# A third context load behind two gathers, and its transposes behind two products

## The chip, the cores and the metric

The kernel runs on one core of a Trainium2 chip. The metric is the device time of one execution in microseconds; shown is the median of three. A profiled execution gives the trace that is read below. PE is TensorE, PEld its weight loads, DVE VectorE, ACT ScalarE, POOL GpSimd, SP SyncE.

## What is computed

A gated block of two parts, each with a layer norm ahead and a residual behind. First each of 2048 tokens goes through one of four experts, chosen by its token id. All three weight matrices of an expert are the same 512 x 512 context block:

```python
def _L0_xattn_ref(hidden_states, token_ids, Wg, Wu, Wd):      # Wg = Wu = Wd = ctx_2048
    expert_ids = jnp.minimum(tid // tokens_per_expert, E - 1)
    for e in range(E):
        g = jax.nn.silu(jnp.einsum('bsd,fd->bsf', hidden_states, Wg[e]))
        u = jnp.einsum('bsd,fd->bsf', hidden_states, Wu[e])
        y = jnp.einsum('bsf,df->bsd', g * u, Wd[e])
        out = jnp.where((expert_ids == e)[..., None], y, out)

x = x + jnp.tanh(g_xattn[0]) * _L0_xattn_ref(_layernorm(x), itok, ctx_2048, ctx_2048, ctx_2048)
x = x + jnp.tanh(g_ffn[0]) * _L0_ffn_ref(_layernorm(x), gate_W, W1, b1, W2, b2)
```

The second part picks two of six experts for each of the four batches and mixes what they give. The change doesn't touch it.

## The kernel before

The program is written by hand, engine by engine: each engine has a list of instructions, runs it strictly in its order, and waits on semaphores. Nothing is scheduled by a planner, so what stands ahead of an instruction in its engine's list delays it.

**Stages.** The kernel first sorts the tokens by expert: 2048 tokens make 19 tiles of up to 128 rows, of which tiles 0 to 3 are the first ones of experts 0 to 3 and the other 15 follow from a table (`te_i`). Then the tile loop computes the first part for each tile and scatters the rows to a scratch in HBM; then four batches of the second part follow. The change lies between the sorting and tile 2.

**Context.** The context of expert e is loaded by SyncE into `raw_ctx[:, e]` (L370, 1 MB each). It is cut into four blocks of 128 columns, n = 4e + k. For each block TensorE makes four transposes into the bank `o_ps[n % 4]` (`transpose_ctx`, L1184), ScalarE copies the bank in reduced precision to `ctx_hi` (`ctx_high`, L940), and VectorE takes the difference of bank and copy to `ctx_lo` (`ctx_low`, L674), so that products can be made as three products of halves. Turning and halving a block is these three steps. `transpose_ctx(n)` for n from 4 waits until block n - 4 is halved, since they share a bank. For blocks 0 and 1 ScalarE does the low half too (`rest_of_ctx`, `ctx_low_alone`).

**Rows.** GpSimd gathers the rows of tiles 0 to 3 by indirect DMAs into `x_ring` (`gather`, L468). For a tile j VectorE makes the statistics (`rows_statistics`, L629 to L631), GpSimd the inverse root (`inverse_root`, L473), VectorE the normalised rows `h` (`normalise`, L651).

**A tile on TensorE.** `transpose_h(j)` (L1114), `first_product(j)` (12 matmuls at L1132: four with both high halves, four with `ctx_lo`, four with `hT_lo`), `transpose_a(j)` (L1123), `second_product(j)` (12 matmuls, the last four with `aT_lo`). Beside them ScalarE copies the high halves (`h_high` L920, `a_high` L925) and makes the silu (`silu_of`, L930); VectorE makes the low halves (`h_low` L657, `a_low` L663), the product with the gate (`up`, L669) and the residual (L636 and on). `invert(o_ps[0], ...)` (L1098) is a product that gives the rows of tiles 4 and later; it uses the bank of block 12 and so waits until that block is halved. VectorE reads its result at L615 to L618, and GpSimd's gather of tile 4 waits for that.

**Loads.** SyncE issues the loads of experts 0, 1 and 2 right at the start and that of expert 3 (`AFTER_ROWS` = E - 1 = 3) once the rows of tile 0 have landed (`gathered[0]`). `warm_up(count)` are transposes of the identity that keep TensorE going and that nobody reads; `WARM[2]` = 9 stand before `transpose_h(0)`, `WARM[3]` = 5 behind it.

Of the kernel before, what the change touches and what calls it, by code (L numbers as in the profile page):

```python
# [74 lines left out]
def flamingo_kernel(nc, x, ids, ctx, g_xattn, g_ffn, gate_w, w1, b1, w2, b2, out):  # L75
    B, S, D = x.shape
    E = ctx.shape[0]
# [9 lines left out]
    AFTER_ROWS = E - 1  # L87
# [29 lines left out]
    with ExitStack() as stack:  # L117
# [3 lines left out]
        def sem(name):  # L121
            return stack.enter_context(nc.semaphore(name))
# [216 lines left out]
        b1_padded, masks_made = sem("b1_padded"), sem("masks_made")  # L339
        half_copied, folded = sem("half_copied"), sem("folded")  # L340
        tiles_landed, warmed = sem("tiles_landed"), sem("warmed")
        ctx_rest_done, ctx_lo_by_act = sem("ctx_rest_done"), sem("ctx_lo_by_act")

        block = stack.enter_context(nc.Block())
# [19 lines left out]
        @block.sync  # L364
        def _(sp):
            sp.dma_start(ids_i[:, :], ids.rearrange("b s -> (b s)").rearrange("(p c) -> p c", c=IDC)).then_inc(ids_here, 16)
            for e in range(E):
                if e == AFTER_ROWS:
                    sp.wait_ge(gathered[0], 16)
                sp.dma_start(raw_ctx[:, e], ctx[e].rearrange("(k p) d -> p k d", p=P)).then_inc(ctx_here[e], 16)  # L370

            for counted in primed:
                sp.sem_inc(counted, 1)

            def load_x1(b):
                for t in range(TT):
                    sp.dma_start(x1_of(b, t * DS, DS),
                                 x1_rows[bass.ds(b * S + t * P, P), :]).then_inc(x1_here[t], 16)

            def load_experts(b):  # L380
                wait_apart(sp, gate_ready, b + 1, waited)
                full = (FC - 1) * P
                chosen = [sp.value_load(top_idx[0:1, s:s + 1], min_val=0, max_val=NE - 1) for s in range(2)]
                one, two = chosen
                first, second = w_raw

                def w1_cols(e, start, stop):
                    return w1[bass.ds(e, 1), :, start:stop].rearrange("o (k p) f -> p (o k) f", p=P)

                def w2_rows(e, start, stop):  # L390
                    return w2[bass.ds(e, 1), start:stop].rearrange("o f d -> (o f) d")

                def w2_blocks(e, start):
                    return w2[bass.ds(e, 1), start:start + full].rearrange("o (c p) d -> p (o c) d", p=P)

                last = slice(W1N + (FC - 1) * D, WN)
                blocks = [raw[:, W1N:W1N + (FC - 1) * D].rearrange("p (c d) -> p c d", d=D) for raw in w_raw]
                if b > 0:
                    sp.wait_ge(lo_done[0], len(PARTS) * b)
                sp.dma_start(part_of(first, 0), w1_cols(one, 0, P)).then_inc(w1_here[0], 16)  # L400
                sp.dma_start(rest_of(first, 0, P + MA), w1_cols(one, P, F2)).then_inc(w1_rest_here[0], 16)
                sp.dma_start(rest_of(first, P + MA, REST), w1_cols(two, 0, MB)).then_inc(w1_rest_here[0], 16)
                sp.dma_start(blocks[0], w2_blocks(one, 0)).then_inc(w2_here[0], 16)
                sp.dma_start(first[0:MA, last], w2_rows(one, full, F2)).then_inc(w2_here[0], 16)
                sp.dma_start(first[MA:P, last], w2_rows(two, 0, MB)).then_inc(w2_here[0], 16)
                if b > 0:
                    sp.wait_ge(lo_done[1], len(PARTS) * b)
                sp.dma_start(part_of(second, 0), w1_cols(two, MB, MB + P)).then_inc(w1_here[1], 16)
                sp.dma_start(rest_of(second, 0, P + LW), w1_cols(two, MB + P, F2)).then_inc(w1_rest_here[1], 16)
                sp.dma_start(blocks[1], w2_blocks(two, MB)).then_inc(w2_here[1], 16)  # L410
                for half in range(2):
                    sp.dma_start(second[half * LW:(half + 1) * LW, last], w2_rows(two, F2 - LW, F2)).then_inc(w2_here[1], 16)
                for e, rows in ((one, (64, 65, 96)), (two, (66, 67, 97))):
                    for row in rows:
                        sp.dma_start(b2_rows[row:row + 1, :], b2[bass.ds(e, 1), :]).then_inc(w2_here[1], 16)

            def store(b):
                for t in range(TT):
                    wait_apart(sp, o_taken, TT * b + t + 2, waited)
                    sp.dma_start(out.rearrange("b s d -> (b s) d")[bass.ds(b * S + t * P, P), :],  # L420
                                 x1_of(b, t * DS, D)).then_inc(out_stored, 16)

            sp.wait_ge(ctxT_done, E * KD)
            sp.wait_ge(tiles_landed, EARLY)
            load_x1(0)
            sp.wait_ge(rows_done, 1)
            sp.wait_ge(pads_made, 2)
            load_experts(0)
            sp.wait_ge(tiles_landed, TILES)
            for b in range(0, B - 1):  # L430
                wait_apart(sp, h2_ready, TT * b + TT, waited)
                wait_apart(sp, out_stored, 16 * TT * b + 1, waited)
                load_x1(b + 1)
                load_experts(b + 1)
                store(b)
            store(B - 1)
            wait_primed(sp, out_stored, 16 * TT * B)
# [3 lines left out]
        def _(pool):  # L441
# [43 lines left out]
                pool.sem_inc(tiles_landed, 1)  # L485

            pool.wait_ge(first_routed, 2)
            for j in range(E):
                gather(j, j)
            inverse_root(0)  # L490
            inverse_root(1)
# [42 lines left out]
        def _(dve):  # L534
# [91 lines left out]
            def rows_statistics(j):  # L626

                dve.wait_ge(gathered[j % RING], 16 * (j // RING) + 16)
                run(dve.bn_stats(stats1[:, :], ring_row(j, 0, D)), apart=True)  # L629
                run(dve.bn_aggr(mv1[:, :], stats1[:, :]))  # L630
                dve.tensor_scalar(ve1[:, :], mv1[:, 1:2], EPS, None, ALU.add).then_inc(ve_ready, 1)  # L631
# [16 lines left out]
            def normalise(j):  # L648
                dve.wait_ge(rstd_ready, j + 1)
                at_least(dve, hT_done, j)  # L650
                dve.tensor_scalar(h[:, :], ring_row(j, 0, D), mv1[:, 0:1], rstd1[:, :],  # L651
                                  ALU.subtract, ALU.mult).then_inc(h_ready, 1)

            def h_low(j):
                dve.wait_ge(hT_hi_done, j + 1)
                hi, lo = hT_of(j)
                dve.tensor_tensor(lo[:, :, :].rearrange("p k t -> p (k t)"), hT_bank(j)[:, :],  # L657
                                  hi[:, :, :].rearrange("p k t -> p (k t)").bitcast(FP32),
                                  ALU.subtract).then_inc(hT_lo_done, 1)
# [7 lines left out]
            def up(j):  # L667
                dve.wait_ge(silu_done, j + 1)
                dve.tensor_tensor(a[:, :], z_bank(j)[:, :], a[:, :], ALU.mult).then_inc(a_ready, 1)  # L669


            def ctx_low(n):
                dve.wait_ge(ctx_hi_done, n + 1)
                dve.tensor_tensor(ctx_lo[:, n * F1:(n + 1) * F1], o_ps[n % 4][:, :],  # L674
                                  ctx_hi[:, n * F1:(n + 1) * F1].bitcast(FP32), ALU.subtract).then_inc(ctx_lo_done, 1)
# [1 line left out]
            for n in range(2, 8):  # L677
                ctx_low(n)
            rows_statistics(0)
            ctx_low(8)  # L680
            normalise(0)
            rows_statistics(1)
            ctx_low(9)
            dve.wait_ge(tg_done, 1)
            h_low(0)
            normalise(1)
            ctx_low(10)
            ctx_low(11)
            h_low(1)
            rows_statistics(2)  # L690
            up(0)
            normalise(2)
            rows_statistics(3)
            dve.wait_ge(ptile_made, 1)
            ones_part = tile_hot[:, :, 1, :]
# [215 lines left out]
        def _(sc):  # L911
# [26 lines left out]
            def ctx_high(n):  # L938
                sc.wait_ge(ctxT_done, n + 1)
                sc.activation(ctx_hi[:, n * F1:(n + 1) * F1], o_ps[n % 4][:, :], ACT.Copy).then_inc(ctx_hi_done, 1)  # L940
# [18 lines left out]
                ctx_high(n)  # L959
            sc.wait_ge(gwT_done, 1)  # L960
            sc.activation(tables[:, :], y_ps[:, 0:TABLES * NE], ACT.Copy).then_inc(gwT_copied, 1)
            for n in range(8, 12):
                ctx_high(n)
            h_high(0)
            h_high(1)
            silu_of(0)
            a_high(0)
            h_high(2)
            silu_of(1)
# [96 lines left out]
        def _(pe):  # L1066
# [141 lines left out]
            for n in range(4, 8):  # L1208
                transpose_ctx(n)
            turn_small_tables()  # L1210
            for n in range(8, 12):
                transpose_ctx(n)

            pe.wait_ge(tg_done, 1)
            warm_up(WARM[2], z_ps)
            transpose_h(0)
            warm_up(WARM[3], z_ps)
            first_product(0, 0, lambda: transpose_h(1))
            first_product(1, 1)
            transpose_a(0)  # L1220
            transpose_h(2)
            transpose_ctx(12)
# [184 lines left out]
```

## Time and profile before

| | us |
|---|---|
| median of three runs (283.15 to 283.76) | 283.19 |
| profiled execution | 283.31 |
| its span, first to last instruction | 281.3 |
| TensorE busy | 275.5 |
| VectorE busy | 216.4 |
| ScalarE busy | 117.1 |
| GpSimd busy | 70.0 |

The span is what the trace shows; 2.0 us of the execution's own time lie around it. A difference in the span is a difference in the time. Busy TensorE time is the sum of matmul records that overlap a little, so what counts is where TensorE waits.

### The profile page before, as it was taken

Reading aid. Unit: us, or ns where it says so; the run is one execution under the profiler, and the core shown is the slowest. Engines: PE = TensorE matmul, PEld = TensorE weight load, DVE = VectorE, ACT = ScalarE, POOL = GpSimd, SP = SyncE. Lnnn points to the kernel's source line nnn. Section 1 sums busy time; section 2 is a strip of 40 time slices with the busy share of each in tenths; the row PEclk is TensorE's granted clock in tenths of the full one; section 3 lists DMA queues with packets and bytes.
Section 4 is the critical chain, followed back from the end, with each engine's and each line's share of the span. In section 5 each row is a group of like instructions: output and inputs, shape, how many; then the busy total and the mean of one; then the engine's idle time right before and its main releaser. Section 6 shows DMA issues by size and latency. Waiting matters only on the chain.

```text
span 281.3 us, 4554 instructions
## 1 busy us (share of the span) xinstructions
PE 275.5 (98%) x1432; PEld 226.3 (80%) x1432; DVE 216.4 (77%) x499; ACT 117.1 (42%) x200; POOL 70.0 (25%) x113
## 2 busy tenths in 40 slices
PE   8999999999999999999999999999999999999995
PEld 7888888888888888787888867888778877888884
DVE  8798988767777899589985768967787677958073
ACT  4745322222222333371628175373644555535020
POOL 5565265555444545222232000000000000000000
PEclk9999999999999999999999999999999999999999
DMA  6870033233355222229513308870196503940003
GB/s 211 287 255 1 6 117 103 78 86 103 81 148 185 76 75 77 75 66 311 170 40 96 129 0 237 239 252 6 51 306 204 171 0 114 317 156 0 0 0 149
DMA packets 24018, 35.00 MB, mean 124 GB/s; under 512 B 4120, under 2 KB 12318, under 8 KB 23996
## 3 DMA queue, kind: packets, MB, share of 16 engines
q1 hardware_dynamic: 20928, 24.72, 28.0%
q0 software_dynamic: 3040, 9.98, 11.6%
q8 instruction: 12, 0.20, 0.3%
q14 instruction: 10, 0.08, 0.1%
q10 hardware_dynamic: 28, 0.02, 0.0%
HBM read 25.52 MB, written 9.19 MB: 123 GB/s over the span
## 4 chain that ended last, share of the span: by engine, by line
PE 91%; DVE 4%; DMA 2%; ACT 1%; issue 1%; POOL 0%; SPq 0%; ACTq 0%
PE bank L1132 35%; PE bank L1106 13%; PE bank L1108 13%; PE bank L1107 13%; PE bank L1114 3%; PE bank L1123 3%; PE bank L1254 2%; DMA raw_ctx<-in_ctx 2%; PE bank L1184 2%; PE bank L1294 1%; PE bank L1325 1%; PE bank L1324 1%; DVE x_odd L842 1%; PE bank L1293 1%; DVE ctx_lo L674 1%; PE bank L1263 1%
## 5 line engine op out<-in xcount | busy, mean ns | idle before, releaser
L1106 PE MATMUL bank<-w_lo,ctx_hi 128*128 128x512 f32 x80 | 32.0, 399 | 0.0
L1108 PE MATMUL bank<-w_hi,ctx_lo 128*128 128x512 f32 x80 | 31.2, 390 | 0.0
L1107 PE MATMUL bank<-w_hi,ctx_hi 128*128 128x512 f32 x80 | 31.2, 390 | 0.0
L930 ACT ACTIVATE a<-bank 128x512 f32<-128x512 f32 x19 | 11.4, 599 | 41.2 <-PE bank L1132 41.2
L995 ACT ACTIVATE w_hi<-w_raw 128x512 fp32r<-128x512 f32 (+3 forms) x24 | 23.9, 1020 | 6.3 <-DMA w_raw<-in_L_ffn_W 6.2
L925 ACT ACTIVATE aT_hi<-bank 128x512 fp32r<-128x512 f32 x18 | 10.8, 598 | 34.3 <-PE bank L1123 34.3
L1002 ACT ACTIVATE act<-bank,tables 128x512 f32<-128x512 f32 x16 | 11.0, 689 | 31.6 <-PE bank L1108 31.4
L1106 PE MATMUL bank<-ctx_lo,w_hi 128*128 128x512 f32 x60 | 23.6, 393 | 0.0
L1132 PE MATMUL bank<-ctx_hi,hT_hi 128*128 (+1 forms) x80 | 23.3, 413 | 0.1
L1107 PE MATMUL bank<-ctx_hi,w_hi 128*128 128x512 f32 x60 | 23.4, 390 | 0.0
L1108 PE MATMUL bank<-ctx_hi,w_lo 128*128 128x512 f32 x60 | 23.3, 389 | 0.0
L468 POOL DMA_INDIRECT x_ring<-in_x,get_rows x19 | 19.1, 1003 | 14.5 <-DVE put_rows L618 9.6
L1132 PE MATMUL bank<-ctx_hi,hT_lo 128*128 (+1 forms) x80 | 21.6, 391 | 0.0
L1132 PE MATMUL bank<-ctx_lo,hT_hi 128*128 (+1 forms) x80 | 21.5, 391 | 0.0
L480 POOL DMA_INDIRECT x_scratch<-x_ring,put_rows x19 | 20.0, 1055 | 5.4 <-POOL x_ring L479 5.4
L663 DVE TENSOR_TENSOR aT_lo<-bank,aT_hi 128x512 fp32r<-128x512 f32 x18 | 12.4, 688 | 10.4 <-ACT aT_hi L925 10.3
L473 POOL TENSOR_TENSOR rstd<-ve,half 128x1 f32<-128x1 f32 x19 | 10.9, 571 | 36.3 <-DVE ve L631 36.3
L1132 PE MATMUL bank<-ctx_hi,aT_hi 128*128 (+1 forms) x72 | 19.8, 396 | 0.0
L1132 PE MATMUL bank<-ctx_hi,aT_lo 128*128 (+1 forms) x72 | 19.6, 392 | 0.0
L834 DVE TENSOR_SCALAR ctx_hi<-act,mix 128x512 fp32r<-128x512 f32 x16 | 7.7, 484 | 15.4 <-ACT act L1002 15.2
L1132 PE MATMUL bank<-ctx_lo,aT_hi 128*128 (+1 forms) x72 | 19.3, 389 | 0.0
L784 DVE TENSOR_TENSOR w_lo<-w_raw,w_hi 128x512 fp32r<-128x512 f32 (+2 forms) x16 | 17.0, 1087 | 1.9 <-ACT w_hi L995 1.8
(214 smaller groups left out, 614.9 us busy)
## 6 DMA issues: line engine op xcount, KB each, us to landing
raw_ctx<-in_ctx SPq DMA_DIRECT2D x4, 1024.0 KB, 7.7
w_raw<-in_L_ffn_W SPq DMA_DIRECT2D x8, 512.0 KB, 4.9
x_even<-x_scratch SPq DMA_DIRECT2D x8, 257.0 KB, 4.1
x_odd<-x_scratch SPq DMA_DIRECT2D x8, 257.0 KB, 3.6
w_raw<-in_L_ffn_W SPq DMA_DIRECT2D x8, 256.0 KB, 3.9
out<-x_even SPq DMA_DIRECT2D x8, 256.0 KB, 2.2
out<-x_odd SPq DMA_DIRECT2D x8, 256.0 KB, 2.1
w_raw<-in_L_ffn_W SPq DMA_DIRECT2D x4, 448.0 KB
```

Of the source, the lines that this page charges most:

```text
L468: pool.indirect_dma_start(x_ring[:, r * DS:r * DS + D], None, x_rows, bass.IndirectOffsetOnAxis(get_rows[:, j:j + 1], 0)).then_inc(gathere ...
L473: pool.tensor_tensor(rstd1[:, :], ve1[:, :], half[:, 0:1], ALU.pow).then_inc(rstd_ready, 1)
L480: pool.indirect_dma_start(x1_rows, bass.IndirectOffsetOnAxis(put_rows[:, j:j + 1], 0), x_ring[:, r * DS:(r + 1) * DS], None).then_inc(scat ...
L663: dve.tensor_tensor(lo[:, :, :].rearrange("p k t -> p (k t)"), bank[:, :], hi[:, :, :].rearrange("p k t -> p (k t)").bitcast(FP32), ALU.su ...
L784: dve.tensor_tensor(part_of(lo, piece), part_of(raw, piece), part_of(hi, piece).bitcast(FP32), ALU.subtract).then_inc(lo_done[s], 1)
L930: sc.activation(a[:, :], z_bank(j)[:, :], ACT.Silu).then_inc(silu_done, 1)
L995: sc.activation(part_of(w_hi[s], piece, s), part_of(w_raw[s], piece, s), ACT.Copy).then_inc(hi_done[s], 1)
L1002: sc.activation(act[:, c % 2, :], hid_ps[k % 2][:, :], ACT.Gelu, bias=b1_of(s, c, slice(0, P), chosen[s])).then_inc(gelu_done, 1)
L1106: pe.matmul(dst, s_hi, m_lo, start=first, stop=False)
L1107: pe.matmul(dst, s_hi, m_hi, start=False, stop=False)
L1108: return pe.matmul(dst, s_lo, m_hi, start=False, stop=last)
L1132: return pe.matmul(dst[:, :], src[:, k, :], weights[:, bass.ds(e * (KD * F1) + k * F1, F1)], start=first, stop=last)
```

## The change

SyncE waits for a new semaphore `rows_asked` before it loads expert 2, and GpSimd raises it once two of the four gathers are issued. On TensorE `transpose_ctx(8)` to `transpose_ctx(11)`, which turn expert 2's context, move from a place ahead of tile 0 to two places, behind `first_product(0)` and behind `first_product(1)`. ScalarE's and VectorE's lists have their `ctx_high` and `ctx_low` of blocks 8 to 11 moved accordingly. No operation is added or taken away but the signal and the wait.

```diff
@@ SyncE
             for e in range(E):
+                if e == AFTER_ROWS - 1:
+                    sp.wait_ge(rows_asked, 1)
                 if e == AFTER_ROWS:
                     sp.wait_ge(gathered[0], 16)
                 sp.dma_start(raw_ctx[:, e], ctx[e].rearrange("(k p) d -> p k d", p=P)).then_inc(ctx_here[e], 16)
@@ GpSimd
             pool.wait_ge(first_routed, 2)
-            for j in range(E):
+            gather(0, 0)
+            gather(1, 1)
+            pool.sem_inc(rows_asked, 1)
+            for j in range(2, E):
                 gather(j, j)
             inverse_root(0)
             inverse_root(1)
@@ VectorE
             for n in range(2, 8):
                 ctx_low(n)
             rows_statistics(0)
-            ctx_low(8)
             normalise(0)
             rows_statistics(1)
-            ctx_low(9)
             dve.wait_ge(tg_done, 1)
             h_low(0)
             normalise(1)
+            h_low(1)
+            rows_statistics(2)
+            ctx_low(8)
+            ctx_low(9)
+            up(0)
+            normalise(2)
             ctx_low(10)
             ctx_low(11)
-            h_low(1)
-            rows_statistics(2)
-            up(0)
-            normalise(2)
             rows_statistics(3)
@@ ScalarE
-            for n in range(8, 12):
-                ctx_high(n)
             h_high(0)
             h_high(1)
+            ctx_high(8)
+            ctx_high(9)
             silu_of(0)
+            ctx_high(10)
+            ctx_high(11)
             a_high(0)
@@ TensorE
             turn_small_tables()
-            for n in range(8, 12):
-                transpose_ctx(n)
-
             pe.wait_ge(tg_done, 1)
             warm_up(WARM[2], z_ps)
             transpose_h(0)
             warm_up(WARM[3], z_ps)
             first_product(0, 0, lambda: transpose_h(1))
+            transpose_ctx(8)
+            transpose_ctx(9)
             first_product(1, 1)
+            transpose_ctx(10)
+            transpose_ctx(11)
             transpose_a(0)
             transpose_h(2)
             transpose_ctx(12)
```

TensorE around tiles 0 and 1, before. `raw_ctx` x16 are the transposes of four blocks, `ident` alone the warm-ups:

```order
L1184 MATMUL bank<-ident,raw_ctx 128x128 x16
L1070 MATMUL bank<-ident 128x128 x9
L1114 MATMUL bank<-ident,h 128x128 x4
L1070 MATMUL bank<-ident 128x128 x5
L1132 MATMUL bank<-ctx_hi,hT_hi 128x512 x4
L1132 MATMUL bank<-ctx_lo,hT_hi 128x512 x4
L1114 MATMUL bank<-ident,h 128x128 x4
L1132 MATMUL bank<-ctx_hi,hT_lo 128x512 x4
L1132 MATMUL bank<-ctx_hi,hT_hi 128x512 x4
L1132 MATMUL bank<-ctx_lo,hT_hi 128x512 x4
L1132 MATMUL bank<-ctx_hi,hT_lo 128x512 x4
```

The 16 transposes stand ahead of the warm-ups and of `h` of tile 0. The same stretch of the changed kernel, whose line numbers are eight higher here:

```order
L1078 MATMUL bank<-ident 128x128 x9
L1122 MATMUL bank<-ident,h 128x128 x4
L1078 MATMUL bank<-ident 128x128 x5
L1140 MATMUL bank<-ctx_hi,hT_hi 128x512 x4
L1140 MATMUL bank<-ctx_lo,hT_hi 128x512 x4
L1122 MATMUL bank<-ident,h 128x128 x4
L1140 MATMUL bank<-ctx_hi,hT_lo 128x512 x4
L1192 MATMUL bank<-ident,raw_ctx 128x128 x8
L1140 MATMUL bank<-ctx_hi,hT_hi 128x512 x4
L1140 MATMUL bank<-ctx_lo,hT_hi 128x512 x4
L1140 MATMUL bank<-ctx_hi,hT_lo 128x512 x4
L1192 MATMUL bank<-ident,raw_ctx 128x128 x8
```

Two groups of eight now stand between and behind the first products. VectorE before, from `up(0)` to `a_low(0)` (`a`, `h`, statistics of tile 3, the three steps for the table of tiles, `aT_lo`):

```order
L669 TENSOR_TENSOR a<-bank,a 128x512
L651 TENSOR_SCALAR h<-x_ring,mv,rstd 128x512
L629 BN_STATS stats<-x_ring 128x6
L630 BN_AGGR mv<-stats 128x2
L631 TENSOR_SCALAR ve<-mv 128x1
L696 TENSOR_TENSOR w_raw<-col_h,ptile 128x16x15
L699 TENSOR_TENSOR w_raw<-col,ends 128x120
L702 TENSOR_TENSOR w_raw<-w_raw,token_h 128x16x15
L663 TENSOR_TENSOR aT_lo<-bank,aT_hi 128x512
```

The same place of the changed kernel, from the statistics of tile 2 on (line numbers six higher):

```order
L680 TENSOR_TENSOR ctx_lo<-bank,ctx_hi 128x512 x2
L675 TENSOR_TENSOR a<-bank,a 128x512
L657 TENSOR_SCALAR h<-x_ring,mv,rstd 128x512
L680 TENSOR_TENSOR ctx_lo<-bank,ctx_hi 128x512 x2
L635 BN_STATS stats<-x_ring 128x6
L636 BN_AGGR mv<-stats 128x2
L637 TENSOR_SCALAR ve<-mv 128x1
L702 TENSOR_TENSOR w_raw<-col_h,ptile 128x16x15
L705 TENSOR_TENSOR w_raw<-col,ends 128x120
L708 TENSOR_TENSOR w_raw<-w_raw,token_h 128x16x15
L669 TENSOR_TENSOR aT_lo<-bank,aT_hi 128x512
```

Four halvings of context blocks came in ahead of `aT_lo`, two of them behind `normalise(2)`.

## Rows read from the trace of the kernel before

**Rows 1.** The page: TensorE's busy time, and the chain by engine.

```profile
PE 275.5 (98%) x1432; PEld 226.3 (80%) x1432; DVE 216.4 (77%) x499; ACT 117.1 (42%) x200; POOL 70.0 (25%) x113
...
PE 91%; DVE 4%; DMA 2%; ACT 1%; issue 1%; POOL 0%; SPq 0%; ACTq 0%
```

**Rows 2.** Who waited for whom, TensorE, whole span: us in total, times, longest.

```profile
PE bank L1114 <- DVE hT_lo L657: 0.7, 1, 0.7
```

**Rows 3.** The chain in order of time: start us, us, what.

```profile
12.79 1.89 DVE ctx_lo L674 x3
...
15.77 0.58 POOL rstd L473
...
16.38 0.56 DVE h L651
...
18.32 2.11 PE bank L1132 x8
...
20.88 3.69 PE bank L1132 x16
...
25.44 0.87 PE bank L1184 x8
...
39.97 0.44 PE bank L1114 x4
```

**Rows 4.** Timeline of TensorE: start us, us, instructions, idle time before.

```profile
4.95 1.85 PE L1070 MATMUL bank<-ident 128*128 128x128 f32 x10
...
13.70 1.97 PE L1184 MATMUL bank<-ident,raw_ctx 128*128 128x128 f32 x16
15.51 1.15 PE L1070 MATMUL bank<-ident 128*128 128x128 f32 x9
16.98 0.66 PE L1114 MATMUL bank<-ident,h 128*128 128x128 f32 x4 [0.33 <-DVE h L651]
```

**Rows 5.** Timeline of VectorE.

```profile
14.59 0.68 DVE L629 BATCH_NORM_STATS2 stats<-x_ring 128x6 f32<-128x512 f32 x1
...
22.15 0.68 DVE L629 BATCH_NORM_STATS2 stats<-x_ring 128x6 f32<-128x512 f32 x1
...
24.45 0.69 DVE L629 BATCH_NORM_STATS2 stats<-x_ring 128x6 f32<-128x512 f32 x1
...
25.45 0.40 DVE L696 TENSOR_TENSOR w_raw<-col_h,ptile 128x240 f16<-128x240 f16 x1
...
26.28 0.68 DVE L663 TENSOR_TENSOR aT_lo<-bank,aT_hi 128x512 fp32r<-128x512 f32 x1
...
36.90 0.69 DVE L629 BATCH_NORM_STATS2 stats<-x_ring 128x6 f32<-128x512 f32 x1 [0.89 <-DMA x_ring<-in_x,get_rows]
```

**Rows 6.** Timeline of GpSimd.

```profile
12.07 0.96 POOL L468 DMA_INDIRECT x_ring<-in_x,get_rows  x1 [0.30 <-issue]
...
14.60 0.95 POOL L468 DMA_INDIRECT x_ring<-in_x,get_rows  x1 [0.31 <-issue]
...
33.33 1.10 POOL L468 DMA_INDIRECT x_ring<-in_x,get_rows  x1 [7.06 <-DVE put_rows L618]
```

**Rows 7.** Instructions at the loads' line, the fourth load alone, the gathers' line (0 to 30 us).

```profile
L370 SPq DMA_DIRECT2D raw_ctx<-in_ctx x4: 368/464/516, 1.2 to 14.3; - x4
...
DMA to landing us min/median/max: 5.7/7.7/10.7
...
raw_ctx<-in_ctx SPq DMA_DIRECT2D x1, 1024.0 KB, 7.4
...
DMA to landing us min/median/max: 4.7/6.0/7.3
```

**Rows 8.** By stretch: busy us of engines (instructions), granted clock, DMA share, GB/s.

```profile
0.00:5.00 5.00, 3.95 (x36) 3.82 (x36) 3.72 (x28) 1.28 (x1) 2.88 (x19) 1.00 0.48 132
5.00:7.00 2.00, 1.89 (x12) 1.66 (x12) 1.97 (x14) 1.66 (x3) 0.94 (x2) 1.00 1.05 402
7.00:17.00 10.00, 9.42 (x95) 8.42 (x95) 8.22 (x27) 7.55 (x15) 5.67 (x7) 1.00 0.78 256
```

More of the change, by code:

```diff
@@ L341, in flamingo_kernel @@
         tiles_landed, warmed = sem("tiles_landed"), sem("warmed")
+        rows_asked = sem("rows_asked")
         ctx_rest_done, ctx_lo_by_act = sem("ctx_rest_done"), sem("ctx_lo_by_act")
```

## Prediction, made before the changed kernel was run

> **What bounds the kernel now.** The page first: TensorE is busy for 275.5 us, 98% of the span, and carries 91% of the chain that ended last [rows 1]. The list of who waited for whom then says how little of TensorE's time is free: over the whole span its longest wait behind the first tile is 0.7 us [rows 2]. So whatever is put on TensorE once the tiles run is paid in full, and whatever moves ahead of them is free as long as TensorE waits there anyway. The question is where that border lies, and the chain in order of time answers it [rows 3]. Tile 0 waits for VectorE to halve context blocks 5 to 7 (from 12.79 us), then for its statistics, GpSimd's root at 15.77 and `h` at 16.38; TensorE turns `h` at 16.98. TensorE itself [rows 4] spends that time on blocks 8 to 11 (16 transposes from 13.70), on nine warm-up transposes from 15.51, and is still 0.33 us too early. Those 16 transposes are no part of the chain. From 16.98 on, TensorE is the chain, bar the copy of `h` on ScalarE.
>
> **The 16 transposes.** The change takes them out of this gap and puts eight behind the first product of tile 0 and eight behind that of tile 1. Eight of them between products take 0.87 us [rows 3], so 2 x 0.87 = 1.74 us join the path. What they leave behind is a wait: nine warm-ups from 13.70 last 1.15 us, to 14.85, and TensorE idles 2.1 us until 16.98.
>
> Can `h` of tile 0 come sooner in return? Hardly. VectorE starts its statistics at 14.59 [rows 5], with no idle time, straight behind block 7 (three halvings in 1.89 us, so one each 0.60). The rows of tile 0 had landed by 14.3, since that is when SyncE's fourth load, which waits for them, goes out [rows 7]. Sooner rows change nothing, as VectorE's list still has all six halvings ahead. And GpSimd issues its fourth gather until 14.60 + 0.95 = 15.55 [rows 6], so with 0.57 for the root and 0.60 for `h` and its hand-over, no ordering gives `h` before about 16.75: the gain is 0.2 us at most, and I take 0. The halving of block 8 that leaves the place before `normalise(0)` lay beside that root and frees nothing. The first product of tile 0 therefore ends where it did: 20.88 + a quarter of 3.69 = 21.80 [rows 3].
>
> **The loads.** The third load now goes out behind the second gather, whose issue ends at 12.07 + 0.96 = 13.03 [rows 6]; with the signal and SyncE's step some 13.2. From issue to landing one load took between 5.7 us (the first, on idle queues) and 10.7 (the third, behind two others); the fourth, beside gathers, took 7.4 [rows 7]. The fourth is the nearest case: landing at 20.6, with 18.9 and 23.9 as ends. It is wanted at 21.80. So it is hidden with 1.2 us to spare, and if that cover is gone it costs up to 2.1. The fourth load follows 1 MB later, 2.6 us at the 402 GB/s of the stretch 5 to 7 [rows 8]: 23.2 us, wanted at about 27.2. Gather 2 goes out at 13.3; the gathers took 4.7 to 7.3 us where loads ran beside them [rows 7], so it lands between 18.0 and 20.6, or at about 23.9 if it sits out both loads. Wanted at 22.15 [rows 5]: hidden. Behind SyncE's new wait stand only the two loads; behind GpSimd's signal stands the third gather, a step that I put at nothing.
>
> The Trainium skill ("DMA: Bandwidth & Descriptors", section "Queues, rings and completion order") says that each DMA engine takes turns between queues packet by packet, by which gather 2 would not sit out both loads. The 7.3 us of the last gather beside a load fits that badly; I keep the late case as a rival.
>
> **VectorE's list.** Here the second cost sits. VectorE is free for tile 2's statistics at 22.15 as before. Before, `a_low(0)` followed at 26.28 [rows 5]. Now blocks 8 to 11 stand in between:
> - statistics 1.01 (those of tile 3 start at 24.45 and the next step at 25.45), so to 23.16, blocks 8 and 9 (1.21, to 24.4), `up(0)` 0.60, `normalise(2)` 0.45: 25.4;
> - block 10 waits for TensorE: 21.80 + 0.87 + 2.77 = 25.43 is the end of tile 1's first product, + 0.44 for the transposes, + 0.60 for ScalarE's copy and its hand-over: 26.5. So VectorE idles 1.1 us, then two halvings: 27.7;
> - statistics 1.01, the three table steps 26.28 - 25.45 = 0.83: `a_low(0)` starts at 29.57 and is out at 30.25.
>
> TensorE: from 25.43, transposes of blocks 10 and 11 to 26.30, of `a` and `h` (0.44 each) and blocks 12 and 13 (0.87) to 28.05, two thirds of the second product (1.84) to 29.89. It then waits for `a_low(0)` until about 30.3: 0.4 us. Next, its product for the table of tiles needs block 12's half. TensorE is there at 30.3 + 0.92 + 0.15 + 0.87 = 32.2. VectorE, behind `a_low(0)`, does `h_low(2)`, `up(1)`, `normalise(3)`, then block 12: 29.57 + 1.81 + 0.45 + 0.68 = 32.5. That is 0.3 us more. Each stop of a running TensorE costs some 0.15 of refill besides (the eight matmuls that start from rest at 18.32 hand over at 20.44, 0.27 more than 8 x 0.23; half of that for a short stop).
>
> Is more late behind this? The rows of tiles 4 and later come from that table, by VectorE's list, which is late by 29.57 - 26.28 = 3.3 us: the gather of tile 4 moves from 33.33 [rows 6] to 36.6. It used to be landed at 36.90 [rows 5], 3.6 us after its issue, so now at 40.2. Statistics 1.01, root and `h` 1.25 give `h` of tile 4 at 42.5. TensorE wants it at 39.97 [rows 3] + 2.7 = 42.7. That just holds; half a microsecond of slip there would cost 0.3. Thereafter the loop runs with the slack that it had.
>
> **Sum.** 1.74 (transposes) + 0.4 (`a_low(0)`) + 0.3 (block 12) + 0.3 (two refills) = 2.7 us. The profiled execution took 283.31 us for a span of 281.3; with 2.7 added, 286.0. The median is 0.12 lower, so 285.9. Bounds of the sum: 1.74 - 0.2 = 1.5 with both waits gone; 1.74 + 1.5 = 3.3 with waits and the slip at tile 4 somewhat larger.
>
> **Rivals.**
> - *Transposes only* (284.9). VectorE's two late steps are later than TensorE by 0.4 and 0.3 us, out of 30; an estimate built from eight terms can be off by as much. For it: 1.1 us of VectorE's idling is in the sum. If halving 10 started 0.5 us sooner, most of the waits would go. Against it: halvings 8 to 11 are 2.4 us of work that was done ahead of 22.15 before.
> - *Late transfers.* The third load lands at 23.9, or gather 2 does. The first makes TensorE stand 2.1 us; VectorE's queue moves with it: 2.7 + 2.1 = 4.8, 288.0. The second moves VectorE's queue by 1.75 less its 1.1 us of idling: 2.7 + 0.7 = 3.4, 286.6. Against it: 7.4 us for the nearest row.
> - *The clock.* The granted clock is 1.00 (2.4 GHz) in every stretch shown [rows 8], through stretches of transposes alone, but no wait behind the first tile is longer than 0.7 us [rows 2] and the new one is 2.1. If it fell to 1.2 GHz for the first product, its 2.77 us would double: 2.7 + 2.8 = 5.5, 288.7. No row shows the lower level, so this is an estimate. The Trainium skill ("TensorE: Matmul & The Clock Gate", "Why this matters for your kernels") warns that a long enough idle gap brings the half rate back; its part 4 adds that transposes don't count as busy, which the 1.00 over seven microseconds of transposes doesn't bear out.
> - *Not slower.* Without the third load in the queues, the context chain before tile 0 could run sooner. Its price has a ceiling: by 7 us 5 x 132 + 2 x 402 = 1464 KB had moved [rows 8], 1049 of them the first load, so even had all the rest been in its way, it would land 415 KB, 1.0 us, sooner. TensorE however runs warm-ups from 4.95 for 1.85 us [rows 4], to 6.8, and the load lands at 1.2 + 5.7 = 6.9 [rows 7]: 0.1 us is left. It would have to save 2.7 to be even and over 2.1 to come within what can be measured. With 0.1 it gives 285.8, so this needs a chain that the rows don't show. Nor can it be that the move does nothing: the built order has the transposes behind the products.
>
> **How the numbers follow.** Forecast 2.7 us (own range 2.3 to 3.3: 285.5 to 286.5): 0.67. Transposes only, 1.5 to 2.3: 0.18. Late transfers: 0.08. Clock: 0.04. Not slower: 0.03, halved between no change and faster. I take 284.7 to 287.0 as the range; it leaves out most of the last three. A measurement of this kernel can tell 0.2%, 0.57 us, from no change; all cases but the last lie beyond it: slower 0.96, same 0.02, faster 0.02.
>
> **What would show it.** Right: TensorE idle about 2.1 us until `h` of tile 0 at 17.0; the second product of tile 0 with a wait for `aT_lo` of some 0.4; the table product with one for `ctx_lo`; every tile from 4 on shifted by about 2.7 at unchanged spacing. Wrong: `h` of tile 0 before 16.7; a wait of TensorE for `raw_ctx`; a granted clock below 1.00 between 15 and 25 us; VectorE idle before `aT_lo` of tile 0; a shift that shrinks or grows behind tile 6.

## The result and the profile after

| | before | changed |
|---|---|---|
| median, us | 283.28 (283.15 to 283.76, 4 runs) | 289.83 (289.41 to 290.22, 4 runs) |
| profiled execution, its span | 283.31, 281.3 | 289.72, 287.8 |

The changed kernel is slower by 6.55 us, a ratio of 1.0219 (in brackets behind a ratio, here and below, its 95% interval: 1.0193 to 1.0246). Slower was forecast, but by 2.7 us: 289.8 lies outside 284.7 to 287.0.

The page of the changed kernel, against [rows 1]. TensorE has 1.9 us more of busy time, and its share of the chain fell from 91 to 88%. In the line of 40 slices its granted clock, which was full everywhere before, has a dent in the third, and the slice itself is three tenths busy:

```profile
PE 277.4 (96%) x1432; PEld 227.6 (79%) x1432; DVE 216.5 (75%) x499; ACT 116.8 (41%) x200; POOL 69.6 (24%) x113
...
PE   8939999999999999999999999999999999999995
...
PEclk9969999999999999999999999999999999999999
...
PE 88%; DVE 6%; DMA 2%; issue 1%; POOL 1%; ACT 1%; ACTq 0%; POOLq 0%
```

Who waited for whom, TensorE, whole span (us in total, times, longest), against [rows 2]:

```profile
PE bank L1122 <- DVE h L657: 4.4, 1, 4.4
...
PE bank L1140 <- DVE aT_lo L669: 0.4, 1, 0.4
PE bank L1106 <- DVE ctx_lo L680: 0.3, 1, 0.3
```

The last two are the waits of the forecast, to the tenth. The first was to be 2.1.

The chain in order of time (start us, us, what), against [rows 3]:

```profile
10.25 0.02 POOLq L493
...
10.50 6.28 DMA x_ring<-in_x,get_rows
...
16.80 0.70 DVE stats L635
...
19.20 1.12 PE bank L1122 x4
...
21.38 2.59 PE bank L1140 x8
...
24.41 0.93 PE bank L1140 x4
25.34 0.87 PE bank L1192 x8
...
46.42 0.44 PE bank L1122 x4
```

Three distances to the kernel before can be read here. `h` of tile 0 is turned at 19.20 instead of 16.98: 2.2 us. The low part of tile 0's first product begins at 24.41 instead of 20.88: 3.5 us, so 1.3 were lost while the same instructions ran. The transposes of `h` at 39.97 stand at 46.42: 6.45 us, so 2.9 were lost in between, and from there on nothing changes up to the end of the span (6.5).

The first distance has its cause at the head of the chain. L493 is GpSimd's signal `rows_asked`, and POOLq is GpSimd's sequencer. The signal was raised at 10.25 us, before the first gather began at 10.50, though it stands behind two gathers in the list. SyncE's list of waits says the same from the other side (first row; up to 10.3 us from about 2.2), and the two transfers that then went out together took 5.8 us (third load) and 6.3 us (gather of tile 0) to land (KB, us to landing):

```profile
SPq L373 <- POOLq L493: 8.1, 1, 8.1
...
raw_ctx<-in_ctx SPq DMA_DIRECT2D x1, 1024.0 KB, 5.8
x_ring<-in_x,get_rows POOLq DMA_INDIRECT x1, 6.3
```

Before, that gather landed by 14.3, 3.7 us after its issue at 10.6. The second distance is the clock. By stretch, with the columns of [rows 8]:

```profile
14.00:15.00 1.00, 0.82 (x8) 0.58 (x6) 0.59 (x1) 0.00 (x0) 0.69 (x2) 1.00 1.10 420
15.00:16.00 1.00, 0.00 (x0) 0.00 (x0) 0.00 (x0) 0.00 (x0) 0.46 (x1) 1.00 1.02 410
16.00:17.00 1.00, 0.00 (x0) 0.00 (x0) 0.20 (x1) 0.00 (x0) 0.00 (x0) 0.51 1.04 336
...
21.00:22.00 1.00, 1.00 (x4) 0.84 (x3) 0.95 (x2) 0.00 (x0) 0.72 (x3) 0.50 0.60 229
22.00:23.00 1.00, 1.00 (x4) 0.79 (x3) 0.24 (x1) 0.00 (x0) 0.77 (x3) 0.57 0.00 0
23.00:24.00 1.00, 1.00 (x7) 0.78 (x6) 0.00 (x0) 0.00 (x0) 0.79 (x3) 1.00 0.00 0
```

TensorE stops at 14.8; at 16 the granted clock goes from 1.00 to 0.50 (from 2.4 to 1.2 GHz), and it stays there until 22.9 (22 to 23 shows 0.57), when a third of the first product is through. The third load, issued early, filled the DMA engines (410 GB/s) while the rows of tile 0 were wanted.

This gave theory A: 2.2 us for the overtaken gather, 1.3 for the clock, 2.9 for what was forecast.

### The profile page after: what moved, and what is told of

Same layout as the page of the kernel before. It is cut to its first block, busy times and chain, and to the rows that moved or that the text cites. A ratio compares the mean times of both kernels' runs of the same rounds, so it can differ in the third digit from the quotient of the medians.

```text
span 287.8 us, 4555 instructions
## 1 busy us (share of the span) xinstructions
PE 277.4 (96%) x1432; PEld 227.6 (79%) x1432; DVE 216.5 (75%) x499; ACT 116.8 (41%) x200; POOL 69.6 (24%) x113
## 3 DMA queue, kind: packets, MB, share of 16 engines
q0 software_dynamic: 3040, 9.98, 11.3%
## 4 chain that ended last, share of the span: by engine, by line
PE 88%; DVE 6%; DMA 2%; issue 1%; POOL 1%; ACT 1%; ACTq 0%; POOLq 0%
PE bank L1140 34%; PE bank L1114 13%; PE bank L1115 12%; PE bank L1116 12%; PE bank L1122 3%; PE bank L1131 3%; DMA x_ring<-in_x,get_rows 2%; PE bank L1263 2%; PE bank L1303 1%; PE bank L1333 1%; PE bank L1334 1%; PE bank L1082 1%; DVE x_odd L848 1%; PE bank L1302 1%; POOL w_raw L468 1%
## 5 line engine op out<-in xcount | busy, mean ns | idle before, releaser
L1140 PE MATMUL bank<-ctx_hi,hT_hi 128*128 (+1 forms) x80 | 24.2, 425 | 0.0
L669 DVE TENSOR_TENSOR aT_lo<-bank,aT_hi 128x512 fp32r<-128x512 f32 x18 | 12.4, 687 | 10.3 <-ACT aT_hi L931 10.3
```

What stands on the lines that cost most here:

```text
L1140: return pe.matmul(dst[:, :], src[:, k, :], weights[:, bass.ds(e * (KD * F1) + k * F1, F1)], start=first, stop=last)
```

## Experiments: taking the three parts apart

Each experiment was timed in three rounds beside the kernel before. The first four ran together; there the kernel before took 283.61 us in the median, but with a scatter from 282.91 to 285.43, so the intervals of these four are wide. The second four ran together too, with 283.23 for it (282.85 to 284.93).

**Order without the loads.** The loads go out as before; only the moved transposes and lists are left.

```diff
-                if e == AFTER_ROWS - 1:
-                    sp.wait_ge(rows_asked, 1)
...
-            gather(0, 0)
-            gather(1, 1)
-            pool.sem_inc(rows_asked, 1)
-            for j in range(2, E):
+            for j in range(E):
                 gather(j, j)
```

> The changed kernel with the loads as before: no wait of SyncE ahead of the third load and no signal; the transposes and the two lists stay moved. Theory A (the 6.5 us are three things: rows of tile 0 landing 2.2 us later because the third load now runs beside their gather, 1.3 us for the granted clock of 0.5 from 16 to 22.5 us, and 2.9 us for the moved transposes with VectorE's list): rows of tile 0 land by 14.3 again, h of tile 0 is turned at 17.0, TensorE idles 2.1 us before it; 286.2 us with the clock held, up to 287.5 if it falls in 2.1 us too. Theory B (the loads are harmless; the moved order costs it all): h of tile 0 at 19.2 or the loss elsewhere, about 289.8.

Measured: 287.84 us (287.23 to 289.00), ratio 1.0148 (1.009 to 1.0207). `h` of tile 0 was turned at 16.76, after a wait of 2.1, as theory A has it. The median is 0.3 above the upper end that it gave; the profiled execution, 287.23, lies inside, and the two slowest of the four (288.26 and 289.00, mean clocks 0.986 and 0.988 against 0.994) have no trace. TensorE's row and the stretches in which its clock fell and rose:

```profile
16.76 1.12 PE L1116 MATMUL bank<-ident,h 128*128 128x128 f32 x4 [2.08 <-DVE h L651]
...
15.00:16.00 1.00, 0.00 (x0) 0.00 (x0) 0.40 (x3) 0.00 (x0) 0.77 (x2) 1.00 0.95 166
16.00:17.00 1.00, 0.24 (x1) 0.24 (x2) 0.84 (x2) 0.00 (x0) 0.12 (x1) 0.78 0.76 231
17.00:18.00 1.00, 1.00 (x6) 1.00 (x6) 0.64 (x3) 0.09 (x1) 0.21 (x1) 0.50 1.05 358
...
19.00:20.00 1.00, 1.00 (x3) 0.73 (x3) 0.80 (x2) 0.00 (x0) 0.74 (x4) 0.52 0.78 293
```

So the wait of 2.1 us that the order alone brings goes with a fall of the clock, for some 3.4 us. Theory B is out: without the loads 2 us of the 6.5 are gone.

**The signal behind the gather.** The same place in GpSimd's list, but raised by an instruction that the engine itself executes.

```diff
+        signal_row = sb("signal_row", [P, 1])
...
-            pool.sem_inc(rows_asked, 1)
+            pool.memset(signal_row[:, :], 0.0).then_inc(rows_asked, 1)
```

> The changed kernel, but the signal for the third load is raised by a one-column memset of GpSimd behind the second gather, not by a semaphore instruction of its sequencer. Theory A (the sequencer's signal overtook both gathers, at 10.26 us, and the load got into the DMA engines ahead of the first gather): the third load goes out at about 13.0, the rows of tile 0 land by 14.3, h of tile 0 is turned at 17.0; 286.2 with the clock held, up to 287.5 if it falls. Theory C (any load amid the gathers delays the first one): rows of tile 0 land after 15.5, the time is 288 or more.

Measured: 287.65 us (287.59 to 287.99), 2.2 below the changed kernel. SyncE now waits three microseconds longer (11.2 instead of 8.1), until the memset at 13.22, and the rows of tile 0 are there when VectorE's list comes to them at 14.79, with no idle time:

```profile
SPq L374 <- POOL signal_row L494: 11.2, 1, 11.2
...
12.27 0.96 POOL L472 DMA_INDIRECT x_ring<-in_x,get_rows  x1 [0.30 <-issue]
13.22 0.12 POOL L494 MEMSET signal_row<- 128x1 f32 x1
...
14.79 0.68 DVE L636 BATCH_NORM_STATS2 stats<-x_ring 128x6 f32<-128x512 f32 x1
...
17.18 0.65 PE L1123 MATMUL bank<-ident,h 128*128 128x128 f32 x4 [2.07 <-DVE h L658]
...
18.00:19.00 1.00, 0.88 (x5) 0.62 (x4) 0.56 (x2) 0.47 (x1) 0.74 (x2) 0.61 1.01 342
...
20.00:21.00 1.00, 1.00 (x4) 0.81 (x3) 0.00 (x0) 0.00 (x0) 0.73 (x4) 0.50 1.01 397
```

That is the whole first distance (the program started tile 0 0.2 us later in this execution, since the first load landed later). Theory C is out. The clock fell here too: the last two rows show a mean of 0.61 in the stretch of its fall and then 0.50.

**The wait filled.** The changed kernel with 46 warm-ups in the place of 9.

```diff
-        WARM = (30, 10, 9, 5)
+        WARM = (30, 10, 46, 5)
```

> The changed kernel with 46 warm-up transposes instead of 9 ahead of h of tile 0, so that TensorE's wait of 4.4 us is filled. Theory A: h of tile 0 still at about 19.2, granted clock 1.00 throughout, first product at full speed; 288.5, that is 1.3 less than the changed kernel. Theory D (the clock's fall is not what the idling does, or transposes don't hold the clock): 0.5 again behind 16 us and 289.8 or a little more.

Measured: 288.00 us (287.93 to 288.15), 1.8 below the changed kernel where 1.3 were expected. TensorE runs through and the clock holds, although all that it runs is transposes:

```profile
13.42 5.24 PE L1078 MATMUL bank<-ident 128*128 128x128 f32 x46
18.65 0.66 PE L1122 MATMUL bank<-ident,h 128*128 128x128 f32 x4
...
14.00:16.00 2.00, 2.00 (x21) 2.00 (x20) 0.39 (x1) 0.00 (x0) 0.95 (x2) 1.00 1.04 407
16.00:18.00 2.00, 2.00 (x21) 2.00 (x20) 1.03 (x3) 0.00 (x0) 0.56 (x1) 1.00 0.86 256
```

Theory D is out. The other 0.5 lies in another place of the profiled execution: the first gather went out 0.2 sooner (10.30 against 10.50) and landed 0.3 sooner after that (statistics at 16.25 against 16.80), so `h` was turned at 18.65 instead of 19.20. What is left of the 1.8 is 1.3 for the clock.

**The loads alone.** The kernel before with SyncE's wait and the sequencer's signal, its order untouched.

```diff
+                if e == AFTER_ROWS - 1:
+                    sp.wait_ge(rows_asked, 1)
...
-            for j in range(E):
+            gather(0, 0)
+            gather(1, 1)
+            pool.sem_inc(rows_asked, 1)
+            for j in range(2, E):
                 gather(j, j)
```

> The kernel before with only the change of loads: SyncE's wait ahead of the third load and the sequencer's signal behind the second gather; transposes and lists as before. Theory A: rows of tile 0 land at 16.8, h of tile 0 is turned at about 19.2; the transposes of blocks 8 to 11 run in the wait for it, from 16.1 on, so nothing of the 2.9 us and little or nothing of the clock: 283.3 + 2.2 = 285.5. Theory B (loads harmless): 283.3.

Measured: 287.79 us (286.25 to 288.49), ratio 1.0115 (1.0055 to 1.0175). Theory B's 283.3 is out, but theory A was short as well. It had `h` right (VectorE made it at 18.56) and TensorE wrong:

```profile
16.12 2.69 PE L1190 MATMUL bank<-ident,raw_ctx 128*128 128x128 f32 x16 [2.25 <-DMA raw_ctx<-in_ctx]
18.60 2.13 PE L1076 MATMUL bank<-ident 128*128 128x128 f32 x9
20.52 0.65 PE L1120 MATMUL bank<-ident,h 128*128 128x128 f32 x4
...
20.00:21.00 1.00, 1.00 (x8) 1.00 (x7) 0.72 (x2) 0.00 (x0) 0.74 (x2) 0.69 1.02 387
```

TensorE stood 2.25 us for the third load, up to 16.1. The clock fell at 17.2 and was back at 20.6 (20 to 21 shows 0.69), so most of the 16 transposes (2.69 us instead of 1.97, [rows 4]) and the nine warm-ups (2.13 instead of 1.15) that stand ahead of `h` in the list ran at the lower level. `h` was turned 3.5 us later than before, 1.3 more than the 2.2 of theory A. The last matmul is late by the same amount (3.6 us), but the span of this execution (286.7 us; its time was 288.49) is 5.4 us longer than before. The other 1.8 us lie behind the last matmul, where SyncE waited 3.5 us for the last store instead of 1.7. Nothing in the trace ties them to the edit, and how much of them is in the median of 287.79 isn't known. In a list that is run in order, warm-ups that once filled a gap are work once the gap is gone.

**The forecast's kernel, twice.** If the two side effects are taken away, what was forecast should be left. Both kernels have 28 warm-ups; one has the loads as before, the other the whole change with the memset's signal.

```diff
-        WARM = (30, 10, 9, 5)
+        WARM = (30, 10, 28, 5)
```

> The changed kernel with the loads as before (no signal, no wait) and 28 warm-up transposes instead of 9 ahead of h of tile 0, so that the 2.1 us in which TensorE stood are filled. Only the moved transposes and lists are left. Theory A: granted clock 1.00, h of tile 0 turned at about 17.0; 1.74 us for the transposes, 0.4 and 0.3 for the two waits of TensorE for VectorE, 0.4 for refills: 286.2 where the kernel before has 283.3. Theory F (the fall of the clock isn't due to TensorE standing still): clock 0.5 again and about 287.5.

> As the last but with the whole change: third load behind a signal that GpSimd raises by a memset after the second gather, and 28 warm-ups. This is the change as it reads, without its two side effects. Theory A: the third load goes out at about 13.1, lands by 21, the first product ends at 21.8; the same 286.2. Theory G (late transfers): TensorE waits for the third load, 287 or more.

Measured: 286.24 us (286.15 to 286.52; ratio 1.0106, 1.009 to 1.0123) and 286.21 us (286.06 to 286.35). Of the first, TensorE's waits and the chain where it leaves TensorE; of the second, `h` of tile 0 behind the warm-ups and the clock beside the third load:

```profile
PE bank L1134 <- DVE aT_lo L663: 0.4, 1, 0.4
PE bank L1100 <- DVE ctx_lo L674: 0.3, 1, 0.3
...
29.77 0.60 DVE aT_lo L663
```

```profile
16.89 0.66 PE L1123 MATMUL bank<-ident,h 128*128 128x128 f32 x4
...
16.00:18.00 2.00, 2.00 (x18) 1.61 (x15) 1.48 (x4) 0.41 (x1) 0.33 (x2) 1.00 1.03 379
```

The two agree within 0.03 us: with a signal in its place, the load among the gathers costs nothing, and it brings nothing either. `a_low(0)` was forecast to start at 29.57; here it is at 29.77, with tile 0 itself 0.1 us later. Theories F and G are out.

**VectorE's list filled.** The first of these two kernels, with the statistics of tile 3 and the table steps moved ahead of the halvings of blocks 10 and 11.

```diff
             normalise(2)
-            ctx_low(10)
-            ctx_low(11)
             rows_statistics(3)
...
             dve.tensor_tensor(tile_hot[:, :, 0, :], ones_part, ..., ALU.mult).then_inc(tile_hot_done, 1)
+            ctx_low(10)
+            ctx_low(11)
             a_low(0)
```

> The kernel of order and 28 warm-ups, with one more edit of VectorE's list: the statistics of tile 3 and the three table steps stand ahead of the halvings of blocks 10 and 11, in the 1.1 us in which VectorE waited for ScalarE's copy. Theory A (VectorE's lateness costs TensorE 1.1 us beside the 1.74): both waits of TensorE go, 1.0 less than the kernel without this edit, 285.2. Theory H (the waits are the late operands' own chain, not VectorE's queue): the same as without the edit.

Measured: 284.99 us (284.82 to 285.40; ratio 1.0063, 1.0046 to 1.008), 1.25 less. Both waits are gone, the chain is TensorE's without a break through tiles 0 and 1:

```profile
21.84 0.87 PE bank L1186 x8
22.72 2.75 PE bank L1134 x12
25.47 0.87 PE bank L1186 x8
26.34 0.44 PE bank L1125 x4
26.78 0.44 PE bank L1116 x4
27.22 0.87 PE bank L1186 x8
28.09 2.74 PE bank L1134 x12
```

What is left is 284.99 - 283.23 = 1.76 us over the kernel before, against 1.74 for two times 0.87 us of transposes. The profiled executions are 2.0 us apart in their spans (283.3 and 281.3), so the agreement to 0.02 is luck; the size is right to some 0.3. Theory H is out.

**Sooner rows from the other side.** An edit of the kernel before: VectorE and GpSimd serve tile 0 first, with the loads untouched.

```diff
-            for n in range(2, 8):
+            for n in range(2, 7):
                 ctx_low(n)
             rows_statistics(0)
-            ctx_low(8)
+            ctx_low(7)
             normalise(0)
+            ctx_low(8)
...
-            for j in range(E):
+            for j in range(E - 1):
                 gather(j, j)
             inverse_root(0)
+            gather(E - 1, E - 1)
             inverse_root(1)
...
-            for n in range(8, 12):
+            for n in range(8, 11):
                 transpose_ctx(n)
-
             pe.wait_ge(tg_done, 1)
             warm_up(WARM[2], z_ps)
+            transpose_ctx(11)
             transpose_h(0)
```

> An edit of the kernel before, towards h of tile 0 sooner without touching the loads: VectorE makes the statistics of tile 0 ahead of the halving of block 7, GpSimd its root ahead of the fourth gather, TensorE turns block 11 behind the warm-ups. The rows of tile 0 land at 14.3 whatever is done, so h can be turned at 16.7 instead of 17.0: 0.3 us less at best, 283.0. If the rows are what bounds it, that is all there is; if VectorE's list alone bounded it, h would come by 16.4.

Measured: 283.22 us (282.84 to 283.39, 10 runs), ratio 0.9994 (0.998 to 1.0008): no difference. VectorE does reach the point at which it waits for the rows, and only for 0.17 us:

```profile
14.37 0.69 DVE L630 BATCH_NORM_STATS2 stats<-x_ring 128x6 f32<-128x512 f32 x1 [0.17 <-DMA x_ring<-in_x,get_rows]
...
16.82 0.66 PE L1116 MATMUL bank<-ident,h 128*128 128x128 f32 x4
```

The gather went out at 10.71 here, so the rows took 3.7 us, and `h` was turned 6.11 us after that issue instead of 6.40 (10.58 to 16.98). The 0.3 us are there and too small to show. No version beat the kernel before.

## Why the prediction was wrong, point by point

The parts, by differences of medians between kernels that differ in one thing:

| part | from | us |
|---|---|---|
| order and lists | 28 warm-ups, loads as before, over the kernel before | 3.0 |
| of it the 16 transposes | with VectorE's list filled, over the kernel before | 1.76 |
| of it VectorE's list | filled against not filled | 1.25 |
| granted clock | signal behind the gather, 9 against 28 warm-ups | 1.4 |
| gather overtaken | changed kernel against the signal behind the gather | 2.2 |

The sum, 3.0 + 1.4 + 2.2 = 6.6, must come out near the 6.55 measured, since the parts are steps of one ladder from the kernel before to the changed one; it is no check, and two of the steps compare a kernel timed with one group against a kernel timed with another. The check is that other ways give much the same. From the turn of `h` to the low part of the first product TensorE took 3.65 us in the kernel before, 4.96 in the changed one, 5.07 with the signal behind the gather and 4.76 in the order alone: 1.1 to 1.4 for the clock. (The order alone gives 287.84 - 286.24 = 1.6 by medians, with the scatter of the first group in it.) With the wait filled in both, the overtaken gather costs 288.00 - 286.21 = 1.8, and 2.0 to 2.2 by the turn of `h` in the traces. For the order and lists the trace of the changed kernel has 2.9.

- **What bounds the kernel**: right. Warm-ups ahead of tile 0 cost nothing as long as they fitted the gap; what was put behind cost its full length.
- **The 16 transposes**, 1.74: right, 1.76 by medians and 2.0 by spans.
- **`h` of tile 0 can't come sooner**: right. The reason was half of it: VectorE's list held `h` up, but by 0.2 to 0.3 us only, and behind it stand the rows, which landed no sooner than 3.7 us after the gather's issue even where the queues had been quiet (signal behind the gather, issue at 10.78).
- **VectorE's list**, 1.0 with refills: right in kind and place, two waits of 0.4 and 0.3; with 1.25 somewhat larger. The sum of this part, 2.7, measured 3.0.
- **The loads** failed, at one step: "The third load now goes out behind the second gather, whose issue ends at 12.07 + 0.96 = 13.03", and "behind GpSimd's signal stands the third gather, a step that I put at nothing". I asked when the gathers' instructions end, and not which part of GpSimd raises the signal. That an engine runs its list strictly in order, as said of the kernel before, did not hold for this step: the sequencer raised the signal at 10.25, without waiting for the gather in front of it. The load went out at 10.3 instead of 13.2, 0.2 ahead of the first gather, which then took 6.3 us instead of 3.7, and the step became a third of the whole loss. The rival *Late transfers* looked at the third load and at gather 2 as victims, never at gather 0, the one that `h` of tile 0 needs.
- **The clock** failed as a term of the sum: it stood there with nothing and among the rivals with 0.04, where the runs showed 1.1 to 1.4 us. The mechanism, the place and the row that would show it were named. In the profiled executions it fell in each of the four kernels that let TensorE stand for 2 us or more in this place, and stayed at 1.00 there in those that filled the wait. The argument against it was that the clock had been full in all stretches shown; but the prediction said itself that none of them held such a wait (the longest was 0.7 us behind the first tile, and 1.0 at the very start), so they bore on nothing. The price of 2.8 was too high, since in the changed kernel the clock was back at 22.9 us, when one third of the product was through. The Trainium skill's sentence on idle gaps ("TensorE: Matmul & The Clock Gate", "Why this matters for your kernels") was the better guide in kind, and the traces agree: waits of 2.1 to 4.4 us brought half the clock. Part 4 of that page of the Trainium skill, by which transposes don't keep the engine busy, is contradicted by 46 of them at 1.00.
- **The range** was drawn around one likely case with two independent side effects, each treated as a rival instead of one that adds. With the wait of 2.1 us certain, the clock's term belonged in the sum. At its own price of 2.8 that gives 288.7, at the measured 1.4 it gives 287.3; the overtaken gather would have been missed either way, and a sum of 288.7 would have come near 289.8 by luck.

## What to carry to other kernels

A signal that is to mean "this DMA is on its way" has to hang on an instruction that the engine itself executes behind it; a bare semaphore step on GpSimd's sequencer ran ahead of two gathers, and a memset behind them, which carries the signal, took the 2.2 us back. When work is taken out of a wait, ask what TensorE does there afterwards: a wait longer than any in the trace is an untested state of the clock, and its term belongs in the sum. And work in a gap is free only until the gap moves: the same kind of warm-ups saved 1.4 us where they filled the new wait, and cost their own length where the rows and the third load were late.

## What the runs showed of the hardware

- GpSimd's sequencer raised a semaphore at 10.25 us that stands behind two indirect DMAs, of which the first was begun at 10.50.
- An indirect gather of 128 rows took 3.7 us to land, both where loads had filled the queues up to 11.3 us (kernel before) and where they had been quiet from 9 us on (signal behind the gather), and 6.3 beside a full 1 MB load issued 0.2 us ahead of it.
- The granted clock fell to 0.50 at 16 us where TensorE had stopped at 14.8; where it stood only from 14.7 to 16.8, it fell as well, and was back some 3.4 us after. Transposes alone, 46 in a row, held it at 1.00, and with the loads alone it came back at 20.6 us while TensorE had run nothing but transposes since 16.1.
- The kernel before, unchanged, scattered in the first comparison: four executions took 282.9 to 283.6 us, with a mean clock of 1.00, and three took 285.2 to 285.4, with 0.996, 0.997 and 0.999. There is no trace of those three, so where the 2 us lie is open. The mean clock doesn't settle it: with 28 warm-ups and the memset it is 0.998 as well, and there the clock is low only in the last stretch (0.52 from 283 us on), behind the last matmul at 281. The profiled execution with the loads alone shows one such place, 1.8 us more behind the last matmul, for the last store.
